# Graph-network setup kernel: the source one-hots made on ScalarE, and two buffers for the rank products

## The reference

```python
edge_index = jnp.stack([src, dst])
x = _layernorm(x + _L0_gnn_ref(x, W, b, w_ih, w_hh, b_ih, b_hh, src, dst, edge_type_4))  # 4 gated steps
x = _layernorm(x + _L1_gnn_ref(x, edge_index, W1a, b1a, W1b, b1b, W2a, b2a, W2b, b2b))   # 2 GIN layers
x = _layernorm(x + _L2_gnn_ref(x, W, b, gamma, beta, edge_index))                        # GCN and batch norm
x = _layernorm(x + _L3_gnn_ref(x, edge_weight, W_self, b_self, W_neigh, b_neigh, src, dst))  # weighted mean
```

## Time and profile before

| what | value |
|---|---|
| median of 3 runs | 9062.16 us (9055.65 to 9072.85) |
| profiled execution | 9078.9 us, its span 9076.7 us |
| busy over the span | PE 73%, DVE 84%, ACT 29%, POOL 53% |
| first and last pair of the setup begin at | 113.3 and 1928.3 us of the span |
| first fold of a pass (PE, L1152) | 2003.6 us |

### The profile page before, as it was taken

The page is one execution under the profiler, slowest core; times in us unless marked ns, Lnnn a source line. Parts: engine busy times, 40 slices in busy tenths (PEclk is TensorE's granted clock), DMA queues, the critical chain, the costliest instruction groups (busy, mean ns, idle before and its releaser), DMA issues.

```text
span 9076.7 us, 299177 instructions
## 1 busy us (share of the span) xinstructions
PE 6665.8 (73%) x121341; PEld 5622.7 (62%) x121342; DVE 7591.1 (84%) x17381; ACT 2638.5 (29%) x6519; POOL 4813.9 (53%) x4224
## 2 busy tenths in 40 slices
PE   3666666658877888788777778876667777748888
PEld 1333333337777777777777767766666667737777
DVE  7988888868887998899788877867779978859998
ACT  0000000003333333333455543321123332234443
POOL 1333333335554564656444447868877767744443
PEclk8888888879999999999888889988889988969999
DMA  2211111136677777777655568988888888848887
GB/s 85 69 48 47 47 47 47 47 93 186 192 190 198 201 201 204 209 202 201 190 162 156 162 185 245 253 243 238 236 236 223 221 232 237 245 120 219 216 218 183
DMA packets 1157755, 1573.98 MB, mean 173 GB/s; under 512 B 407396, under 2 KB 850695, under 8 KB 1153466
## 3 DMA queue, kind: packets, MB, share of 16 engines
q1 hardware_dynamic: 916698, 898.54, 37.5%
q10 hardware_dynamic: 126656, 482.46, 15.2%
q0 software_dynamic: 113056, 174.29, 9.8%
HBM read 990.67 MB, written 564.09 MB: 171 GB/s over the span
## 4 chain that ended last, share of the span: by engine, by line
DVE 45%; PE 20%; DVEq 12%; DMA 9%; issue 9%; POOL 3%; ACT 2%; SPq 1%; ACTq 0%; POOLq 0%
DVE work L1983 7%; DMA work<-bounce_f 4%; DVE work L1958 3%; DMA bounce_f<-work 3%; DVE work L1939 3%; DVEq L1965 3%; POOL work L972 3%; DVE hs L1949 2%; DVE work L1745 2%; PE ps_gate L1244 2%; DVE work L1978 2%; PE ps_agg L1054 2%; DVE work L1866 2%; DVE hs L1737 2%; PE ps_agg L1183 2%
## 5 line engine op out<-in xcount | busy, mean ns | idle before, releaser
L972 POOL DMA_INDIRECT work<-node_rows,work x3528 | 4154.3, 1178 | 2753.9 <-issue 1254.4
L1183 PE MATMUL ps_agg<-work 120*128 120x64 bf16 (+1 forms) x12544 | 1394.9, 199 | 550.3 <-DVE work L1983 536.2
L1183 PEld LDWEIGHTS ps_agg<-work 120*128 120x128 bf16 x12544 | 1213.2, 102 | 599.8 <-issue 598.0
L1184 PE MATMUL ps_agg<-work 120*128 120x64 bf16 x12544 | 1392.6, 199 | 18.5 <-issue 18.0
L1185 PE MATMUL ps_agg<-work 120*128 120x64 bf16 x12544 | 1395.5, 199 | 11.5 <-issue 11.4
L1184 PEld LDWEIGHTS ps_agg<-work 120*128 120x128 bf16 x12544 | 1202.6, 102 | 35.6 <-issue 23.2
L1185 PEld LDWEIGHTS ps_agg<-work 120*128 120x128 bf16 x12544 | 1200.6, 101 | 18.2 <-issue 17.9
L1978 DVE TENSOR_TENSOR work<-work 120x1024 f32<-120x1024 f32 x784 | 956.3, 1220 | 305.1 <-DMA work<-bounce_f 301.6
L1152 PE MATMUL ps_pair<-rows_now,work 128*128 128x64 bf16 x26112 | 1008.6, 198 | 146.4 <-DMA work<-src_onehots 57.9
L1939 DVE TENSOR_TENSOR work<-iota_bf,dl_all 120x2048 bf16<-120x2048 bf16 x882 | 1075.0, 1219 | 15.3 <-POOL rows_now L998 7.3
L1205 PE MATMUL ps_agg<-work 128*128 128x64 bf16 (+1 forms) x23520 | 928.3, 195 | 178.1 <-DMA work<-node_rows,work 127.7
(11 more groups left out here) (345 smaller groups left out, 13037.5 us busy)
## 6 DMA issues: line engine op xcount, KB each, us to landing
bounce_f<-work ACTq DMA_DIRECT2D x816, 480.0 KB
work<-bounce_f SPq DMA_DIRECT2D x784, 480.0 KB
work<-src_onehots SPq DMA_DIRECT2D x918, 256.0 KB
bounce<-work ACTq DMA_DIRECT2D x102, 727.5 KB
work<-bounce SPq DMA_DIRECT2D x98, 727.5 KB
work<-node_rows,work POOLq DMA_INDIRECT x3528
work<-grid_vals SPq DMA_DIRECT2D x49, 960.0 KB, 5.0
node_rows<-stage SPq DMA_DIRECT2D x686, 48.0 KB
```

The lines of the kernel that those rows point to most:

```text
L972: pool.indirect_dma_start(out=ring[:, at.slot6() * LB + b, 0:3 * H], out_offset=None, in_=table_of(at.p), in_offset=bass.IndirectOffsetOnA ...
L1183: mm(acc[:, to:to + n], hot, low[at.two()][0:ROWS, b, 0:n], start=b == 0, stop=False)
L1184: mm(acc[:, to:to + H], hot, tops(rest_f[at.two()])[0:ROWS, b, :], start=False, stop=False)
```

## The change

1. `src_hot` moves from DVE to ACT. There it takes `Square(lo - (lane + 1))` of all of `lo_two` in place (128x3840, one instruction, with the new column `lane_off` as bias), and then `Relu(1 - square)` into `oh_all` as fp8, in eight instructions of 480 elements. ACT does it between `copy_ranks(q)` and `copy_slots(q)`, in a loop that is now unrolled six times. The wait for `src_hot_stored` stands before the first `Relu`.
2. DVE keeps the two `dl_all` instructions (`keep_dst`).
3. The rank products get a buffer each, `prods[0]` and `prods[1]`. `rank_in_lower(1)` stands directly behind `rank_in_lower(0)`, and the wait for `rank_folded[0]` between them is gone.
4. To find room, `win` and `lo_two` move to `hs`, `before` to `turned`, `grid_now` to `stage` and `x_left` to `extra`, tiles that have room while the pairs are sorted.
5. SP waits for `lo_used` (now counted by ACT) before it loads `lo_two` again, before `store_hot`, and once for `rows_moved`.

```diff
     hot_b = c.take(WC * NCLS, bf16)
-    before = c.take(NCLS, bf16), c.take(NCLS, bf16)
-    prod = c.take(WC * NCLS, bf16)
+    prod, prod_b = [c.take(WC * NCLS, bf16) for _ in range(2)]
...
-    x_left = [c.take(XC * H, fp32).rearrange("p (d f) -> p d f", f=H) for _ in range(2)]
+    win = [c.take(2 * WC * REC, fp32).rearrange("p (t n f) -> p t n f", t=2, f=REC) for _ in range(2)]
+    lo_two = c.take(2 * TILE_SLOTS, bf16)
...
+    grid_now = stage[:, :, :, :].rearrange("p a b f -> p (a b f)")[:, 0:2 * WC * GM].rearrange(
+        "p (t n v u) -> p t n v u", t=2, n=WC, u=SLOTS)
+    turned_bf = turned[:, :].bitcast(bf16)
+    before = [turned_bf[:, a * NCLS:(a + 1) * NCLS] for a in range(2)]
+    x_left = [extra[:, :, :].rearrange("p a f -> p (a f)")[:, a * XC * H:(a + 1) * XC * H]
+              .rearrange("p (d f) -> p d f", f=H) for a in range(2)]
...
-        def store_hot(g):
-            sp.wait_ge(src_hot_made, g + 1)
+        def store_hot(g, last=False):
+            sp.wait_ge(lo_used, WPAIRS if last else g * 3 + 3)
             sp.sem_inc(sp_ran, 1)
             sp.dma_start(src_onehots.ap()[ds(g * P, P), :], oh_all_words
                          ).then_inc(src_hot_stored, 16)
...
                 store_left(q - 1)
+                if not (known and q == 1):
+                    sp.wait_ge(lo_used, q - 1)
+                    sp.sem_inc(sp_ran, 1)
                 load_back(q - 1)
             if u % 3 == 1 and not (known and q < 4):
                 store_hot(i * 2 + (u // 3 - 1))
...
+        sp.wait_ge(dst_used, WPAIRS - 1)
         load_back(WPAIRS - 1)
         store_hot(GROUPS - 2)
-        store_hot(GROUPS - 1)
+        store_hot(GROUPS - 1, True)
         sp.wait_ge(src_hot_stored, 16 * GROUPS)
         sp.wait_ge(left_stored, 16 * WPAIRS)
         sp.wait_ge(first_stored, 16)
...
+        def src_hot(q, j, waits):
+
+            lo_tiles = lo_two.rearrange("p (t u i n) -> p t u i n", t=2, u=SLOTS, i=NI)
+            oh_tiles = oh_all[:, :, 0:ROWS].rearrange("p (i b) (j n u) -> p i b j n u", b=SB, j=G_TILES, n=K)
+            act.wait_ge(lo_back, q * 32 + 32)
+            act.sem_inc(act_ran, 1)
+            a_(lo_two, lo_two, ACT.Square, bias=lane_off[:, :]).then_inc(lo_squared, 1)
+            act.wait_ge(lo_squared, q + 1)
+            act.sem_inc(act_ran, 1)
+            if waits is not None:
+                act.wait_ge(src_hot_stored, waits)
+                act.sem_inc(act_ran, 1)
+            for t in range(2):
+                for k in range(K):
+                    last = a_(oh_tiles[:, :, :, j + t, k, :],
+                              lo_tiles[:, t, :, :, k * SB:(k + 1) * SB].rearrange("p u i b -> p i b u"),
+                              ACT.Relu, bias=ones_f[:, 0:1], scale=-1.0, saturate=False)
+            last.then_inc(lo_used, 1)
+
+        def windows(i, u, known):
+            q = i * 6 + u
+            copy_ranks(q)
+            if not (known and q < 2):
+                waits = (i * 2 + (u // 3)) * 16 if u % 3 == 2 and not (known and q < 3) else None
+                src_hot(q - 2, 2 * ((u + 1) % 3), waits)
+            copy_slots(q, known and q == 0)
+
         for u in range(6):
             for n in range(2 * u, min(2 * u + 2, NT // XC)):
                 x_middle(n)
-            copy_ranks(u)
-            copy_slots(u, u == 0)
+            windows(0, u, True)
         act.wait_ge(x_low, NT // XC)
         act.dma_start(rows_of(0), rows_now[:, :, :]).then_inc(first_stored, 16)
-        with act.Fori(6, WPAIRS) as q:
-            copy_ranks(q)
-            copy_slots(q, False)
+        with act.Fori(1, 8) as i:
+            for u in range(6):
+                windows(i, u, False)
+        windows(8, 0, True)
+        src_hot(WPAIRS - 2, G_TILES - 2, None)
+        src_hot(WPAIRS - 1, 0, 16 * (GROUPS - 1))
         act.wait_ge(setup_done, 1)
 
...
                 dve.wait_ge(rank_copied[t], q + 1)
-                v.tensor_tensor(prods, hot[t], before[t].rearrange("p (o c) -> p o c", o=1)
+                v.tensor_tensor(prods[t], hot[t], before[t].rearrange("p (o c) -> p o c", o=1)
                                 .to_broadcast([P, WC, NCLS]), ALU.mult).then_inc(sums_picked[t], 1)
...
             rank_in_lower(0)
+            rank_in_lower(1)
             v.tensor_tensor(same, key.rearrange("p t (n o) -> p t n o", o=1).to_broadcast([P, 2, WC, WC]),
                             key.rearrange("p t (o n) -> p t o n", o=1).to_broadcast([P, 2, WC, WC]), ALU.is_equal)
             dve.drain()
             v.tensor_tensor(same, same, earlier.to_broadcast([P, 2, WC, WC]), ALU.mult)
             dve.drain()
             v.tensor_reduce(out=ahead, in_=same, axis=AX.X, op=ALU.add)
-            dve.wait_ge(rank_folded[0], q + 1)
-            rank_in_lower(1)
             if spare_work is not None:
                 spare_work()
...
-        def src_hot(q, j, waits):
+        def keep_dst(q):
 
             dve.wait_ge(lo_back, q * 32 + 32)
-            if waits is not None:
-                dve.wait_ge(src_hot_stored, waits)
             dve.sem_inc(dve_ran, 1)
-            lo_tiles = lo_two.rearrange("p (t u i n) -> p t u i n", t=2, u=SLOTS, i=NI)
-            oh_tiles = oh_all[:, :, 0:ROWS].rearrange("p (i b) (j n u) -> p i b j n u", b=SB, j=G_TILES, n=K)
             for t in range(2):
-                v.tensor_scalar(dl_all[0:ROWS, ds(q * 2 + t, 1), :].rearrange("p j (n o) -> p (j n) o", o=2),
-                                dst_two[0:ROWS, t, :].rearrange("p (n o) -> p n o", o=1).to_broadcast([ROWS, GB, 2]),
-                                room_all[0:ROWS, ds(q * 2 + t, 1)], None, ALU.mult)
-                for k in range(K):
-                    last = v.tensor_scalar(oh_tiles[:, :, :, j + t, k, :],
-                                           lo_tiles[:, t, :, :, k * SB:(k + 1) * SB].rearrange("p u i b -> p i b u"),
-                                           lane1_col[:, :], None, ALU.is_equal, saturate=False)
-            if j == G_TILES - 2:
-                last.then_inc(src_hot_made, 1)
-            dve.drain().then_inc(lo_used, 1)
+                last = v.tensor_scalar(dl_all[0:ROWS, ds(q * 2 + t, 1), :].rearrange("p j (n o) -> p (j n) o", o=2),
+                                       dst_two[0:ROWS, t, :].rearrange("p (n o) -> p n o", o=1).to_broadcast([ROWS, GB, 2]),
+                                       room_all[0:ROWS, ds(q * 2 + t, 1)], None, ALU.mult)
+            last.then_inc(dst_used, 1)
 
         def windows(i, u, known):
             q = i * 6 + u
 
             def spare_work():
-                waits = (i * 2 + (u // 3)) * 16 if u % 3 == 2 else None
-                if known and q < 3:
-                    waits = None
-                src_hot(q - 2, 2 * ((u + 1) % 3), waits)
+                keep_dst(q - 2)
 
             rank_pair(q, i * 3 + (u // 2 + 1), u % 2, known and q == 0, None if known and q < 2 else spare_work)
...
         mend_left(WPAIRS - 1)
-        src_hot(WPAIRS - 2, G_TILES - 2, None)
-        src_hot(WPAIRS - 1, 0, 16 * (GROUPS - 1))
-        dve.drain().then_inc(src_hot_made, 1)
+        keep_dst(WPAIRS - 2)
+        keep_dst(WPAIRS - 1)
```

More of the change, by code:

```diff
@@ L185, in build @@
     c = Carver(work[:, :], WORK)
-    lo_two = c.take(2 * TILE_SLOTS, bf16)
     oh_all = c.take(NS * P, fp8).rearrange("p (s q) -> p s q", q=P)
@@ L189, in build @@
     dst_two = c.take(2 * GB, bf16).rearrange("p (t n) -> p t n", t=2)
-    win = [c.take(2 * WC * REC, fp32).rearrange("p (t n f) -> p t n f", t=2, f=REC) for _ in range(2)]
     hot_b = c.take(WC * NCLS, bf16)
-    before = c.take(NCLS, bf16), c.take(NCLS, bf16)
-    prod = c.take(WC * NCLS, bf16)
+    prod, prod_b = [c.take(WC * NCLS, bf16) for _ in range(2)]
     key_i, lane_i = [c.take(4 * WC, i16).rearrange("p (t n o) -> p t n o", t=2, o=2) for _ in range(2)]
@@ L203, in build @@
     places = c.take(2 * WC * SLOTS, fp32).rearrange("p (t n u) -> p t n u", t=2, u=SLOTS)
-    grid_now = c.take(2 * WC * GM, bf16).rearrange("p (t n v u) -> p t n v u", t=2, n=WC, u=SLOTS)
     left_now = c.take(2 * WC * RECS * LV, bf16).rearrange("p (t n b v) -> p t n b v", t=2, n=WC, b=RECS)
@@ L214, in build @@
     hot = [t.rearrange("p (n c) -> p n c", c=NCLS) for t in (c.take(WC * NCLS, bf16), hot_b)]
-    x_left = [c.take(XC * H, fp32).rearrange("p (d f) -> p d f", f=H) for _ in range(2)]
+    win = [c.take(2 * WC * REC, fp32).rearrange("p (t n f) -> p t n f", t=2, f=REC) for _ in range(2)]
+    lo_two = c.take(2 * TILE_SLOTS, bf16)
     lane_hot = [prod[:, a * WC * P:(a + 1) * WC * P].rearrange("p (n c) -> p n c", c=P) for a in range(2)]
-    prods = prod.rearrange("p (n c) -> p n c", c=NCLS)
+    prods = [x.rearrange("p (n c) -> p n c", c=NCLS) for x in (prod, prod_b)]
     counts = sb("counts", [P, NT, K + 1], fp32)
@@ L365, in build @@
     lo_used = sem("lo_used")
-    src_hot_made = sem("src_hot_made")
+    dst_used = sem("dst_used")
+    lo_squared = sem("lo_squared")
     src_hot_stored = sem("src_hot_stored")
```

(3 more changed lines are left out.)

2 lines of the change are left out of this document (added).

## The result

| what | before | after |
|---|---|---|
| median of 4 runs | 9060.19 us | 8800.18 us (8782.62 to 8813.72) |
| ratio after / before | | 0.971, 95% interval 0.9687 to 0.9732 |
| profiled execution, its span | 9078.9, 9076.7 us | 8790.8, 8789.0 us |
| one pair of tiles in the setup | 37.81 us | 31.80 us (forecast 32.4) |
| first fold of a pass | 2003.6 us | 1718.6 us |

The setup is 285.0 us shorter. The rest of the span, from the first fold of a pass on, is 7073.1 us before and 8789.0 - 1718.6 = 7070.4 after: nothing was won or lost there.

What follows compares the result with a forecast made beforehand. DVE, busy 89% in the loop over pairs, was taken as the bound. 47 pairs x 5.4 = 254 and 6.5 us gained, 5 and 3.5 lost: 252 off 9078.9 gives 8827, or 8810 for the median (range 8775 to 8910).

Steps and rivals of the forecast that it cites:

- DVE's work, 4.5 us a pair: In each pair, moving the one-hots off DVE takes 4.5 us of work from it; the `dl_all` instructions keep 0.40.
- The wait for `ps_turn` goes: DVE's idle 0.97 us before the second rank product goes, 44.6 us in 49 waits; first product to second sum becomes 10.7.
- The second fold at the fast level: PE's fold of tile 1 takes 3.09 us, after only 0.6 us idle, so a pair gains 5.4 us.
- Rival A: PE's fold of tile 1 stays at the slow level: 139 us gained, 8923 us; chance 0.10.
- ScalarE hidden: ACT's one-hots take 8.4 us a pair, end 6.8 us before the grid copy is due, and cost nothing.
- The cover, "from 15 us each further us costs up to one us": If ACT takes 15 us in a pair its cover is gone, and each further us costs up to one per pair.
- Rival B: ScalarE becomes the bound, deciding from 15 us a pair, gain cancelled at 20.6: 191 us lost, 9253 us; chance 0.05.
- The end, 3.5 us lost: At the setup's end, ACT takes 8.4 us instead of 4.9 for pair 47's one-hots: 3.5 lost; pair 48 costs 0.
- Clock of the rank copies: DVE's wait for the first rank copy, 46.8 us in 37 of 49 pairs, could change by -47 to +15; taken as 0.
- POOL, 5 us lost: POOL's small instructions may fall beside DVE's second product: 0.1 us a pair, 5 us lost (bounds 0 and 12).
- First two pairs: These have no one-hots; the fold of tile 1 moves forward 3.2 us, so 6.5 us is gained in two pairs.
- Rival C: The gain goes into another wait, PE's grid placing or SP's stores; a pair keeps 37.8 us: 9062 us; chance 0.02.

Runs made afterwards that it cites:

- experiment 1: Changed kernel with the source one-hots put back on DVE behind both rank products: ratio to the kernel before 0.994, pair 36.48 us, setup 1937.4 us.
- experiment 2: Changed kernel with one buffer for both rank products and the old DVE order, one-hots on ACT: ratio to the kernel before 0.9983, setup 1981.6 us.
- experiment 4: Changed kernel with ACT's eight `Relu`s of a pair done three times: ratio to the kernel before 1.0037, pair 37.23 us, setup 2028.0 us.
- experiment 3: Changed kernel with ACT's eight `Relu`s of a pair done twice: ratio to the kernel before 0.974, pair 32.08 us, setup 1749.5 us.
- experiment 8: The changed kernel again, unaltered, on another chip: ratio to the kernel before 0.9768, pair 31.89 us, setup 1721.6 us.
- experiment 6: Changed kernel with the two `dl_all` instructions of each pair on ACT behind the `Relu`s: pair 31.98 us, setup 1727.1 us, no ratio given.
- experiment 7: Changed kernel with `dl_all` on ACT and the last two pairs' one-hots on DVE: ratio to the kernel before 0.976, setup 1705.4 us.

## Why the prediction was right, step by step

- **DVE's work, 4.5 us a pair: right.** 4.51 measured.
- **The wait for `ps_turn` goes: right,** 43.8 us to none. The stretch is 10.81 us long, forecast 10.7.
- **The second fold at the fast level: right.** This was the step that could fail most. Experiments 1, 2 and 4 show it from three sides: at most 0.82 us idle ahead, always fast; 3.85 ahead, 547 ns in the median; 2.3 to 7.7 ahead, slow even for the other tile's fold. Rival A fell by this. The reason given, the idle time just ahead, holds for the folds; as a rule for all of PE's bursts it fails, as the rank sums below show.
- **ScalarE hidden: right, but for a cost that was mis-sized.** The `Relu` was estimated from dense rows. The dense form does take 683 ns in the mean, but the real one reads with a stride and takes 1137, so the share is 12.0 us and not 8.4. The Trainium skill, "ScalarE: Activation LUTs", What ACT_TABLE_LOAD costs, gives 280 ns + 0.833 ns an element for every function with a bias column, 680 ns here (an estimate from its figures). The trace agrees for dense input and not for the strided one. By the 0.3 us and 0.83 ns that the prediction took from that page, the share comes to 3.5 + 8 x 0.70 = 9.1 us, not to about 8.4; nothing hung on it. The prediction also doubted that DVE is the faster engine for this work. It is, with 0.58 us for 480 elements against 1.04 from start to start: the move pays because ACT's time is hidden, not because ACT is quick.
- **The cover, "from 15 us each further us costs up to one us": wrong.** At 20.5 us the pair lost 0.2, not 5.5. The reckoning took the grid copy for due when it used to come. Its consumers had slack too (experiment 3), and the limit is ACT's whole chain against DVE's pair, by the estimate of experiment 4 at about 24 us. (Rival B's 15 + 5.4 is 20.4, not 20.6.)
- **The end, 3.5 us lost: mis-sized, 10.4.** The same `Relu` error, twice, at the one place where nothing covers it.
- **Clock of the rank copies, taken as 0 between -47 and +15: 24.7 us were won.** This is the largest part of the 36 us between the forecast of the profiled execution (8827) and what it took (8790.8). The traces show where it comes from. DVE's wait goes with the level of PE's first rank sums of the pair, 18 products of 384 columns. Where they take 3.10 us, DVE waits 0.08 at most; where they take 4.4 to 5.9, it waits 0.6 to 2.3. They are slow in 37 of 49 pairs before (46.8 us of wait) and in 15 after (22.1). Why fewer are slow isn't shown, and the idle time just ahead doesn't explain it: in 20 of the 37 it is under 2 us, while after the change 29 of the 34 fast ones have more than 2.3 us idle ahead. Two neighbouring pairs of experiment 1 show both:

```profile
1759.29 4.78 PE L1065 MATMUL ps_agg<-hs,above 128*128 128x384 bf16 x18 [1.63 <-DVE hs L1775]
1795.54 3.10 PE L1065 MATMUL ps_agg<-hs,above 128*128 128x384 bf16 x18 [2.69 <-DVE hs L1775]
```

The number of slow pairs also shifts with small edits: 18 for the same kernel in experiment 8, 20 and 13 in experiments 6 and 7, 29 with the buffers alone. The prediction had no ground for the sign of this term, so that it helped is luck.

- **POOL, 5 us lost: nothing.** The medians of the two products are 3758 and 3800 ns, and were 3816 and 3758. POOL's own busy time rises from 590 to 763 us over the pairs; nobody waits for it.
- **First two pairs, 6.5: 7.2 won.** The wait of 8.1 us is 0.9. **Larger loop body, 0: right.** The loop's turns on DVE are 21.0 and 21.5 us.

The 36 us are, besides the 24.7 of the rank copies: 5.0 that POOL did not cost, 4.7 in idle time of DVE that no wait is named for, 2.8 more from DVE's work and `ps_turn` together, 2.7 in the passes, 1.5 more from the wait for `ps_gate`, and 0.5 before the first pair; the last pair and the end together take 6.0 back. Besides the clock no term of the sum is off by more than 7 us. Rival C, another wait in place of the gain, fell for the change as a whole. It is what happens to the one-hots' half by itself (experiment 2).

## What to carry to other kernels

Work that an engine does beside another engine's result is also the cover of that result. Before moving it off, find which wait ends behind it, and move the producer forward in the same change, or most of the gain turns into that wait (22 us for the move alone, 282 with the reordering). An engine's cost estimated from dense rows holds for dense reads alone, and it matters first where the work is not covered, at the end of the loop.
